# One reduction split in two, four half-width passes merged into full-width ones, in the quantization of the hidden layer

## The reference

```python
def _quant_act(x):
    scale = 127.0 / jnp.clip(jnp.max(jnp.abs(x), axis=-1, keepdims=True), EPS, None)
    xq = jnp.clip(jnp.round(x * scale), -128.0, 127.0) / scale
    return x + jax.lax.stop_gradient(xq - x)

def _bitlinear(x, w):
    return jnp.einsum('bsi,oi->bso', _quant_act(x), _quant_weight(w))

h = jax.nn.gelu(_bitlinear(x, w1), approximate=False)   # 1024 -> 4096
return _bitlinear(h, w2)                                # 4096 -> 1024
```

## Time and profile before

| what | us |
|---|---|
| median of 2 runs | 4706.71 (4701.84 to 4711.58) |
| the profiled execution, its own time | 4741.77 |
| its span, slowest core (core 3) | 4740.2 |
| span of the fastest core (core 6) | 4654.6 |

### The profile page before, as it was taken

One profiled execution on the slowest core, in us unless ns is written; L12 is line 12 of the kernel. 1 busy time (PEld: TensorE's weight loads), 2 busy tenths in 40 slices (PEclk: granted clock), 3 DMA queues, 4 the chain that ended last, 5 costly groups with the idle time before them and its releaser, 6 DMA issues. The chain is left out here.

```text
span 4740.2 us, 41104 instructions; the slowest of 8 cores (4654.6 to 4740.2 us)
## 1 busy us (share of the span) xinstructions
PE 2785.9 (59%) x12088; PEld 1543.5 (33%) x12088; DVE 2980.6 (63%) x2882; ACT 1718.2 (36%) x2181; POOL 224.7 (5%) x406
## 2 busy tenths in 40 slices
PE   3000266666666664555555555555555459999998
PEld 2000255555555541222222222222222124444444
DVE  5541477777776664888888888888888812232222
ACT  0000144444444433555555555555555401111111
POOL 1000000000000000000000000000000000000000
PEclk7555677877777666777777777777777779999999
DMA  7889411111111112122212212221211166666665
GB/s 244 237 228 112 136 54 54 54 54 58 66 55 54 52 47 109 51 60 62 62 61 62 62 51 60 62 63 61 62 56 58 49 173 155 152 151 152 155 149 131
DMA packets 467197, 447.35 MB, mean 94 GB/s; under 512 B 405008, under 2 KB 405008, under 8 KB 456224
## 3 DMA queue, kind: packets, MB, share of 16 engines
q0 software_dynamic: 68384, 344.04, 21.7%
q1 hardware_dynamic: 398592, 100.68, 13.6%
HBM read 193.02 MB, written 150.99 MB: 73 GB/s over the span
## 5 line engine op out<-in xcount | busy, mean ns | idle before, releaser
L859 PE MATMUL ps_h<-w1T,qdT 128*128 128x512 bf16 x4096 | 1034.9, 420 | 971.9 <-DMA qdT<-qd 971.9
L859 PEld LDWEIGHTS ps_h<-w1T,qdT 128*128 128x128 bf16 x4096 | 429.3, 106 | 1577.5 <-issue 1195.8
L971 PE MATMUL ps_f<-w2T,qhT 128*128 128x512 bf16 x4096 | 887.0, 380 | 74.6 <-DMA qhT<-qhscr 74.6
L147 ACT ACTIVATE h_b<-ps_h,zerov,g3s 128x512 f32<-128x512 f32 x512 | 398.1, 778 | 517.5 <-PE ps_h L859 517.5
L971 PEld LDWEIGHTS ps_f<-w2T,qhT 128*128 128x128 bf16 x4096 | 401.4, 98 | 560.2 <-issue 78.9
L674 PE MATMUL ps_u<-lnT,winT 128*128 128x256 f32 x2048 | 400.6, 379 | 217.2 <-ACT gu L147 179.1
L674 PEld LDWEIGHTS ps_u<-lnT,winT 128*128 128x128 f32 x2048 | 387.8, 290 | 235.7 <-issue 234.0
L147 DVE BATCH_NORM_STATS2 bn<-ffn 128x6 f32<-128x512 f32 x128 | 88.8, 694 | 584.0 <-ACT ffn L147 577.1
L147 DVE TENSOR_REDUCE amh<-h_b 128x1 f32<-128x4096 f32 x64 | 282.9, 4420 | 254.6 <-ACT h_b L147 254.6
L147 ACT ACTIVATE y0h<-h_b,halfv,sch_all 128x2048 f32<-128x2048 f32 x128 | 267.9, 2093 | 364.6 <-DVE sch_all L147 358.6
L662 PE MATMUL ps_t<-identt,ln1f 128*128 128x128 f32 x512 | 94.2, 340 | 479.8 <-ACT ln1f L147 373.3
(11 more groups left out here) (109 smaller groups left out, 2509.5 us busy)
## 6 DMA issues: line engine op xcount, KB each, us to landing
wstg<-w POOLq DMA_DIRECT2D x32, 2048.0 KB, 10.0
qhscr<-qh_b POOLq DMA_DIRECT2D x64, 1024.0 KB, 5.1
x_buf<-x POOLq DMA_DIRECT2D x32, 1024.0 KB, 6.4
r2scr<-r2b POOLq DMA_DIRECT2D x64, 512.0 KB, 3.0
r2B<-r2scr POOLq DMA_DIRECT2D x64, 512.0 KB, 5.8
r2C<-r2scr POOLq DMA_DIRECT2D x64, 512.0 KB, 5.4
y<-outb POOLq DMA_DIRECT2D x64, 512.0 KB, 3.0
wstg<-w_in POOLq DMA_DIRECT2D x2, 2048.0 KB, 13.3
```

Source lines behind the costliest of these rows:

```text
L147: ins = f(*a, **k)
L859: last = t.matmul(ps_h[q % 6][:], qdTv[ta % 2][:, j, :], w1v[:, j, 512 * hs:512 * (hs + 1)], start=(j == 0), stop=(j == DT - 1))
L971: last = t.matmul(pslice, qhTv[ta % 2][:, j, :], w2v[:, j, 512 * half:512 * (half + 1)], start=(j == 0), stop=(j == HT - 1))
```

## The change

In DVE's queue the reduction of `h_b` becomes two, each 2048 wide: the first waits for four gelus and writes a new tile `amh0`, the second waits for all eight and writes `amh`; a one-column `tensor_tensor` takes the larger of the two. DVE's eight correction passes 2048 wide become four passes 4096 wide, behind one wait for `s_r16h`. In ACT's queue the four half-width instructions (`y0h`, `r16h`, `y0h`, `r16h`) become two full-width ones, and `s_r16h` is raised once. `s_qh` too is raised once per tile, and the waits for it on POOL and ACT are counted anew. Nothing else is touched.

```diff
+            amh0 = sb1("amh0", [128, 1], F32)
...
-                    g.wait_ge(sem("s_qh"), 2 * ta + 2)
+                    g.wait_ge(sem("s_qh"), ta + 1)
...
+                    v.wait_ge(sem("s_gel"), HS * ta + HS // 2)
+                    v.tensor_reduce(amh0[:], h_b[:, 0:H // 2], axis=AX.X,
+                                    op=ALU.max, apply_absolute_value=True)
                     v.wait_ge(sem("s_gel"), HS * ta + HS)
-                    v.tensor_reduce(amh[:], h_b[:], axis=AX.X,
+                    v.tensor_reduce(amh[:], h_b[:, H // 2:H], axis=AX.X,
                                     op=ALU.max, apply_absolute_value=True)
+                    v.tensor_tensor(amh[:], amh[:], amh0[:], op=ALU.max)
...
                     if ta + 1 < NT2:
                         dcorr(ta + 1)
-                    for hf in range(2):
-                        hsl = slice(2048 * hf, 2048 * (hf + 1))
-                        v.wait_ge(sem("s_r16h"), 2 * ta + hf + 1)
...
+                    v.wait_ge(sem("s_r16h"), ta + 1)
+                    v.tensor_tensor(bh[:], y0h[ta % 2][:], r16h[ta % 2][:],
+                                    op=ALU.is_lt)
+                    v.scalar_tensor_tensor(ch[:], y0h[ta % 2][:], 1.0,
+                                           r16h[ta % 2][:],
+                                           op0=ALU.subtract, op1=ALU.is_ge)
+                    v.tensor_tensor(bh[:], ch[:], bh[:], op=ALU.subtract)
+                    if ta >= 2:
+                        v.wait_ge(sem(f"s_qhd{ta % 2}"), 16 * (ta // 2))
+                    iqh = v.scalar_tensor_tensor(qh_b[ta % 2][:], r16h[ta % 2][:],
+                                                 385.0, bh[:],
+                                                 op0=ALU.subtract, op1=ALU.add)
+                    inc("s_qh", iqh)
...
-                            a.wait_ge(sem("s_qh"), 2 * (tb - 1))
-                        for hf in range(2):
-                            hsl = slice(2048 * hf, 2048 * (hf + 1))
...
+                            a.wait_ge(sem("s_qh"), tb - 1)
+                        a.activation(y0h[tb % 2][:], h_b[:], AF.Identity,
+                                     bias=halfv[:], scale=sch_all[:, tb:tb + 1])
+                        irh = a.activation(r16h[tb % 2][:], y0h[tb % 2][:],
+                                           AF.Identity, bias=zerov[:], scale=1.0)
+                        inc("s_r16h", irh)
```

## The result

| | before | after |
|---|---|---|
| median of the runs, us | 4714.29 (10 runs) | 4658.43 (11 runs) |
| ratio, 95% interval | | 0.9883 (0.9861 to 0.9904) |
| the profiled execution, us | 4741.77 | 4658.43 |
| its slowest core's span, us | 4740.2 (core 3) | 4656.9 (core 5) |
| first to last scale on that core, us | 1936.5 | 1872.8 |

The account below looks back on a forecast made before the run. B1 was taken as bound by a cycle of waits through PE, then by DVE's queue: 63 x 29.68 plus 3 of hiccups, 1873 instead of 1936.5. With the ends -63, so 4706.7 - 63 = 4644 us, range 4612 to 4682.

Parts of the forecast that it names:

- A round of 30.74 that hangs on the cycle through PE: B1 before: scale, `dcorr`, DMA, PE, gelu, reduction in turn set each of 63 rounds, 30.74 us.
- The prices of the new widths: Wider DVE and ACT instructions, extrapolated on a line: 4.42, 2.29, 3.80, 3.71 us; half reduction 2.29.
- Rival 1: Wider DVE and ACT passes cost in proportion, so only gaps are saved: 4673 to 4716 us; chance 0.07.
- The new wait of DVE: DVE before `bh`: waiting for ACT's full-width pair adds 3.09 us of idle time a round.
- T: The end of a scale in B1, from which times within a round are counted.
- The split: DVE's reduction: first half from T+23.95 to T+26.24, second from T+26.34, after the last gelu at T+25.36.
- The later signals: POOL and ACT: `r2B` starts 1.19 us after the corrections' end with 6.7 to spare; `r16d` done about T+10.4.
- The round: B1 after: DVE's own queue sets the pace at 29.68 us a round, instead of 30.74.
- hiccups: Occasional DVE gaps of 0.4 to 0.5 us where 0.1 is usual: some eight, +3 us in B1.
- Rival 2: B1: the cycle through PE stays the bound and the full 1.87 us a round arrives, 4589 us; chance 0.05.
- Rival 3: PE's bursts run longer at 1.2 GHz, 0.2 us extra per cold matmul, eating the gain: above 4707; chance 0.04.
- the ends: Outside B1's rounds: first scale 1.87 us sooner, last tile 2.36 later, together +0.5.

Follow-up runs that it names:

- merge_only: The changed kernel with the one 4096 wide reduction of before, all passes full-width: 4708.94 us, ratio 0.9996 to the kernel before.
- before_ahead: The kernel before with only the dense tile scaled and corrected one tile further ahead: 4492.74 us, ratio 0.9568.
- mix_ahead: The kernel before with the dense tile one further ahead and only the last two pairs of DVE's correction passes merged: 4445.77 us, ratio 0.9456.
- split_only: The kernel before with the reduction split in two as in the change and nothing merged: 4614.71 us, ratio 0.9775.
- after_ahead: The changed kernel with the dense tile scaled and corrected one tile further ahead: 4654.48 us, ratio 0.9889 to the kernel before.
- after_pe8: The changed kernel with the first of each tile's eight blocks of matmuls computed twice, eight matmuls more per burst: 4707.62 us in one execution.
- act_halves: The changed kernel with ACT's four half-width instructions of before, DVE still waiting for both halves: 4708.05 us in one execution.
- split_late: The kernel before with the reduction split unevenly, 3072 columns after six gelus and 1024 after all eight: 4532.11 us, ratio 0.9626.

## Why the prediction was right

The prediction held: 4644 forecast, 4658 measured, a ratio of 0.9867 (4644 to 4706.7) against 0.9883 with its interval from 0.9861. The mechanism was right, and not only the number. Step by step:

- **A round of 30.74 that hangs on the cycle through PE.** Right. `merge_only` delays DVE by 2.04 within the round and the round stays; `before_ahead` takes PE off the cycle and the round falls to DVE's own sum, worked out ahead as 27.12 and measured as 27.16.
- **The prices of the new widths.** On the line: 4425, 2292, 3800, 3707 and 2286 ns, where I had 4.42, 2.29, 3.80, 3.71 and 2.29. The small `tensor_tensor` took 160 ns and not 150. Rival 1 is out. The measured pair of passes in `before_ahead` and `mix_ahead` also decides against 75 ns an instruction, the figure that the Trainium skill gives (Vector Engine (DVE) Microarchitecture Reference, Measured stream behaviour on trn2).
- **The new wait of DVE.** `bh` at T+7.98 forecast, T+7.99 measured; 3.09 beyond the usual tenth, 3.19 with it.
- **The split.** First half from T+23.95 forecast, T+23.97 in the timeline; second half without a wait.
- **The later signals.** The load `r2B` starts 1.18 after the corrections' end (1.19 forecast), and `r16d` is done at T+10.39 (10.4 forecast). Neither holds anything up. PE's wait for `qdT` is 13.6, as forecast.
- **The round.** 29.68 without hiccups, and 29.73 with them; measured 29.73. 63 rounds 1873 forecast, 1872.8 measured.
- **Rival 2**, the cycle through PE as the bound and 1.87 gained: it is what `split_only` is, 1.74 gained. In the changed kernel it is out, as `after_ahead` shows.
- **Rival 3**, PE's clock: it had more substance than I gave it, and did not decide. I held against it that the bursts are as long as before. They are so on average only. Two neighbours in the trace after, and one earlier burst:

```profile
2028.63 16.91 PE L855 MATMUL ps_h<-w1T,qdT 128*128 128x512 bf16 x64 [13.29 <-DMA qdT<-qd]
...
3009.20 16.44 PE L855 MATMUL ps_h<-w1T,qdT 128*128 128x512 bf16 x64 [13.77 <-DMA qdT<-qd]
...
3038.90 15.25 PE L855 MATMUL ps_h<-w1T,qdT 128*128 128x512 bf16 x64 [13.26 <-DMA qdT<-qd]
```

  The number of matmuls at 1.2 GHz at the head of a burst goes from 6 to 14 after, where it was 9 to 11 before in all rounds but the first (13). On core 5 the last gelu ended at T+26.08 at the latest; the second half reduction wanted it at T+26.29 or later. I had worked out a slack of 1.0 from the mean, and had left out that a reduction which waits starts 0.17 behind its gelu, so that it was 0.8 by my own numbers. In the closest round nothing of it was left. That round is on core 6: the gelu ends at 2374.84, and the second half reduction, which is the latter half of the bar, starts at 2375.02, 0.18 later.

```profile
2372.63 4.67 DVE L147 TENSOR_REDUCE amh<-h_b 128x1 f32<-128x2048 f32 x2
...
2374.06 0.78 ACT L147 ACTIVATE h_b<-ps_h,zerov,g3s 128x512 f32<-128x512 f32 x1 [0.95 <-PE ps_h L855]
```

  It was enough in each of the 63 rounds on each of the eight cores, but that it always was is partly luck: the forecast knew the mean of the bursts and not their spread.
- **The profiled execution.** Forecast at 4679, it took 4658.4. The forecast carried over the 35 us by which the profiled execution of the kernel before lay above the median, and this one lies on the median. The miss is not of the mechanism.
- **The last 8 us** of the difference (63 against 55) are not settled. The rounds give 63.7, the ends took a little more than I had: from the last scale to the end of the span it is 971.5 after and 967.7 before, 3.8 longer where I had 2.4. The rest lies within the ratio's interval, which reaches from 45 to 66 us.

## What to carry to other kernels

Ask of each part of a combined change what idle time pays for it: here the split and the merge both spent the same 3.5 us of DVE's idle time before the reduction, and only the first had a return. Keep passes narrow where they start on fresh data of another engine, and merge those further down the queue, whose data is there anyway (26.65 in `mix_ahead`, against 29.72 in `after_ahead`, of which the split reduction is 0.52). And take an engine that waits for its input half the time off the cycle by preparing that input one tile further ahead, before anything is tuned on the engine that feeds it (30.74 to 27.16). Where each instruction waits for the one before it, one that is dropped gives back its gap and its whole fixed part, 0.25 us here on DVE.

## What the hardware showed that I had not expected

How much of a burst runs at 1.2 GHz changes with when the burst starts, and where the round hangs on PE that moves the next start. In the kernel before, 1.2 GHz holds for 9 to 11 matmuls of a burst, round after round but the first; in `after_pe8` for 9 to 11 and in `merge_only` for 10 to 12. All three rounds hang on PE and are 30.71 to 30.74 long. That they are equally long needs no cause in the clock: before and `merge_only` have the same cycle through PE, and in `after_pe8` a later gelu and a shorter second reduction add up to 30.7 (27.2 + 0.17 + 2.29 + 1.05).

In the other kernels the number wanders, between 6 and 14. `act_halves` shows that the length alone does not decide: its round of 30.59 is nearly as long, DVE sets its pace, and its number creeps from 6 or 7 up to 14 and falls back. `split_only` hangs on PE and alternates. Three bursts of it, core 5, with 14, 9 and 14 matmuls at 1.2 GHz:

```profile
3013.95 16.84 PE L864 MATMUL ps_h<-w1T,qdT 128*128 128x512 bf16 x64 [12.68 <-DMA qdT<-qd]
3043.45 15.76 PE L864 MATMUL ps_h<-w1T,qdT 128*128 128x512 bf16 x64 [12.66 <-DMA qdT<-qd]
3072.02 16.82 PE L864 MATMUL ps_h<-w1T,qdT 128*128 128x512 bf16 x64 [12.81 <-DMA qdT<-qd]
```

The second starts 29.50 after the first and has 9, the third 28.57 after the second and has 14: the burst that comes 0.9 us sooner lasts 1.1 us longer, and makes the next one late. That goes on through all 63 rounds. Whether the clock takes back part of a gain is a matter of the average, and the average differs: 10.3 matmuls before, 11.0 in `split_only`, whose gain came out 0.13 short, but 9.6 in `split_late`. These are readings of the rounds; no run changed the clock alone to test them.
